# A state-space scan with gated output and attention: y, rows and gate loaded at other places of the loop, mixing split in two

## The reference, cut to what matters

```python
xn = (xc - mu) / jnp.sqrt(var + 1e-05) * ln_g + ln_b        # xc: conv and silu of x @ W_in
Bm, Cm, dt = jnp.split(xn @ W_xproj.T, 3, axis=-1)
def step(h, inputs):
    ad, bd, xt, ct = inputs
    h = jnp.clip(h * ad[:, :, None] + bd[:, :, None] * xt[:, None, :], -10.0, 10.0)
    return h, jnp.einsum('bd,bdh->bh', ct, h)
_, ys = jax.lax.scan(step, h0, (Ad, Bd, xn, Cm))
y = ys + D * xn
x = x + y * jax.nn.silu(gate) @ W_out.T
x = x + attention_layer(x)
```

## Time and profile before

| | us |
|---|---|
| median of 3 runs | 2897.28 |
| lowest, highest | 2895.61, 2928.46 |
| the profiled execution | 2895.71 |
| its span | 2893.9 |
| scan, first to last VectorE step | 466.6 to 1454.99 |

### The profile page before, as it was taken

The page is one execution under the profiler, slowest core; times in us unless marked ns, Lnnn a source line. Parts: engine busy times, 40 slices in busy tenths (PEclk is TensorE's granted clock), DMA queues, the critical chain, the costliest instruction groups (busy, mean ns, idle before and its releaser), DMA issues. The chain is left out here.

```text
span 2893.9 us, 55595 instructions
## 1 busy us (share of the span) xinstructions
PE 2689.5 (93%) x20489; PEld 1466.8 (51%) x20490; DVE 2001.7 (69%) x2112; ACT 1189.3 (41%) x2039; POOL 1281.7 (44%) x583
## 2 busy tenths in 40 slices
PE   7999955999999999999979999969999999999999
PEld 3444333666666665666657777833333333333337
DVE  2788867987888878888853333366777677676726
ACT  2677762221222212122132122126666666666641
POOL 0000002655555555555541222026667777777763
PEclk9999967999999999999989999979999999999999
DMA  3246576878887888888744444372344354354347
GB/s 106 88 154 219 181 257 142 186 164 156 165 162 168 165 155 157 159 162 166 156 141 165 139 143 158 142 200 66 74 110 111 89 128 108 95 126 118 81 173 228
DMA packets 260356, 424.01 MB, mean 147 GB/s; under 512 B 59440, under 2 KB 127664, under 8 KB 253824
## 3 DMA queue, kind: packets, MB, share of 16 engines
q1 hardware_dynamic: 177920, 332.86, 44.5%
q10 hardware_dynamic: 82304, 89.44, 12.7%
HBM read 260.91 MB, written 163.08 MB: 147 GB/s over the span
## 5 line engine op out<-in xcount | busy, mean ns | idle before, releaser
L939 DVE CUSTOM_DVE_ANT_0 b_h<-b_h,b_bx,b_bounds_all 128x512 f32<-128x512 f32 x1024 | 825.7, 806 | 167.1 <-PE b_bx L1087 118.0
L1643 DVE TENSOR_REDUCE e_half_max<-ef_banks 128x4 f32<-128x2048 f32 x256 | 586.3, 2293 | 233.3 <-PE ef_banks L1596 233.3
L1786 POOL TENSOR_TENSOR e_pair_sum<-e_probs 128x2048 f32<-128x2048 f32 x128 | 585.7, 4576 | 264.9 <-PE ef_banks L1635 215.1
L1755 ACT ACTIVATE e_probs<-ef_banks 128x512 f32<-128x512 f32 x1024 | 555.7, 595 | 309.9 <-PE ef_banks L1610 309.9
L1610 PE MATMUL ef_banks<-e_qs,e_ks 97*128 97x512 f32 x1024 | 382.0, 452 | 3.9 <-DVE e_half_max L1643 3.6
L1143 ACT COPY d_v_rows<-b_y_psum 128x128 f32<-128x128 f32 x256 | 67.9, 265 | 690.3 <-PE b_y_psum L1097 690.3
L1087 PE MATMUL b_bx<-b_x_moving,b_b_weights 24*128 24x512 f32 x1024 | 260.4, 504 | 78.1 <-DMA b_x_moving<-xn_parts 46.7
L1610 PEld LDWEIGHTS ef_banks<-e_qs,e_ks 97*128 97x128 f32 x1024 | 154.5, 188 | 330.9 <-ACT e_probs L1755 312.4
L1067 POOL TENSOR_TENSOR b_b_weights<-b_bd,b_mask_b 128x512 fp32r<-128x512 f32 x64 | 82.4, 1287 | 512.9 <-POOLq L861 462.8
L1097 PE MATMUL b_y_psum<-b_h,b_c_weights 128*32 128x128 f32 x8224 | 279.8, 277 | 0.5 <-ACT d_v_rows L1143 0.5
L1620 PE MATMUL ef_banks<-e_probs,e_v 128*32 128x512 f32 x2048 | 273.6, 606 | 0.4 <-ACT e_probs L1755 0.4
(11 more groups left out here) (225 smaller groups left out, 4105.8 us busy)
## 6 DMA issues: line engine op xcount, KB each, us to landing
b_x_moving<-xn_parts SPq DMA_DIRECT2D x252, 128.0 KB
e_ks<-qk_parts ACTq DMA_DIRECT2D x42, 512.0 KB, 4.9
e_qs<-qk_parts ACTq DMA_DIRECT2D x84, 256.0 KB, 3.4
xn_full<-a_xn SPq DMA_DIRECT2D x32, 512.0 KB, 3.3
xn_parts<-a_hi SPq DMA_DIRECT2D x64, 256.0 KB, 2.5
xn_parts<-a_lo SPq DMA_DIRECT2D x64, 256.0 KB, 2.5
silu_gate<-d_v_rows ACTq DMA_DIRECT2D x64, 256.0 KB, 5.6
shared<-xn_full SPq DMA_DIRECT2D x128, 128.0 KB, 5.9
```

The lines of the kernel that those rows point to most:

```text
L939: return nc.vector._custom_dve(bass.dve_ops.TENSOR_ADD_SAT, **operands)
L1643: nc.vector.tensor_reduce(out=half_max[:, u // UNITS % 2, :, r // NH, r % NH], in_=(banks[:, u % 2 * GROUP:(u % 2 + 1) * GROUP] if u < FIR ...
L1755: nc.scalar.activation(probs[:, g % 4, h, :], p_exp[h % 2], ACT.Exp).then_inc(exps, 1)
L1786: nc.gpsimd.tensor_tensor(out=pair_sum[:, t % 2], in0=probs[:, (2 * t) % 4], in1=probs[:, (2 * t + 1) % 4], op=ALU.add).then_inc(paired, 1)
```

## The change

SP: load_y handles tile it-2 and stands behind load_moving half 0 and load_bd; it additionally waits for `gated` of the tile before. load_xn moves from there to a place behind load_sg, after the loads of half 1. GpSimd: mix is cut into scale_rows (xn * D), add_y (plus y) and gate_rows (times the gate). scale_rows of tile it-1 stays at the end of the iteration; add_y and gate_rows of tile it-2 come between split_low and low_turned of the same tile. The ends of the loops follow. In the phase before, spread_early stands at the end of a round and not at the start of the next.

```diff
--- before.py
+++ after.py
@@ -343,8 +343,6 @@
                 for b in range(BATCH):
                     pj.load_style(sp, b)
                 pj.load_others(sp)
-            if p >= 2:
-                spread_early(sp, p - 2)
             if p >= 1:
                 store_b(sp, p - 1, 0, b_hi)
                 store_b(sp, p - 1, 1, b_lo)
@@ -359,6 +357,8 @@
                         for j in "wu":
                             pj.load_mat(sp, mat_of[j], j)
                 store_inverse(sp, p)
+            if 1 <= p <= 2:
+                spread_early(sp, p - 1)
 
         def in_proj(pe, n, m):
             i = n * NM + m
@@ -923,6 +923,7 @@
                 sp.wait_ge(sg_out[half], START + j * 16 + 16)
             sp.dma_start(sg_in, SG[bass.ds(j, 1)].rearrange("o p c -> (o p) c")).then_inc(sg_back, 16)
         def load_y(sp, j):
+            sp.wait_ge(gated, START + j)
             for i in range(2):
                 sp.wait_ge(y_out[i], START + j * 64 + 64)
             for b in range(BATCH):
@@ -938,13 +939,14 @@
         def add_clipped(**operands):
             return nc.vector._custom_dve(bass.dve_ops.TENSOR_ADD_SAT, **operands)
 
-        def mix(e, engine, j):
-
+        def scale_rows(e, engine, j):
             e.wait_ge(xn_in, START + j * 64 + 64)
             engine.tensor_tensor(out=xn, in0=xn, in1=d_row, op=ALU.mult).then_inc(mixed, 1)
+        def add_y(e, engine, j):
+            e.wait_ge(y_in, START + j * 64 + 64)
             e.wait_ge(mixed, START + j * 2 + 1)
-            e.wait_ge(y_in, START + j * 64 + 64)
             engine.tensor_tensor(out=xn, in0=xn, in1=y[:], op=ALU.add).then_inc(mixed, 1)
+        def gate_rows(e, engine, j):
             e.wait_ge(mixed, START + j * 2 + 2)
             e.wait_ge(sg_back, START + j * 16 + 16)
             e.wait_ge(turned, START + j * 2)
@@ -1024,14 +1026,13 @@
 
 
 
-        def sp_loop(sp, it, store=True, x=True, more=True, load_d=False):
-            j = it + (-1)
+        def sp_loop(sp, it, y=True, store=True, more=True, load_d=False):
             sp.wait_ge(read, START + it * PAIRS + 8)
             load_moving(sp, it, 0)
             sp.wait_ge(w_ready[1], START + it * 2 + (-1))
             load_bd(sp, it, 1)
-            if not load_d:
-                load_xn(sp, j)
+            if y:
+                load_y(sp, it + (-2))
             sp.wait_ge(read, START + it * PAIRS + 16)
             load_moving(sp, it, 1)
             if more:
@@ -1041,40 +1042,42 @@
             if load_d:
                 sp.wait_ge(out_split, START + 4)
                 sp.dma_start(d_row, I["D"].rearrange("(o n) -> o n", o=1).to_broadcast([P, INNER])).then_inc(out_in, 16)
-                load_xn(sp, j)
-            load_sg(sp, j)
-            load_y(sp, j)
+            load_sg(sp, it + (-1))
+            load_xn(sp, it + (-1))
             if store:
-                store_x1(sp, j + (-2))
-            if x:
-                load_x(sp, j + (-1))
-
-
-        def pool_loop(pool, it, j, out=False, split=True, low=False, split_out=False):
-            for i in range(2):
-                if i == 1 and split:
-                    split_low(pool, it)
-                if i == 1 and split_out:
-                    for c in range(4):
-                        out_low_part(pool, c)
-                if i == 1 and low:
-                    low_turned(pool, j + (-1), 0)
-                t0 = it * STEPS + i * T
-                pool.wait_ge(read, START + it * PAIRS + (10 + 8 * i))
-                pool.wait_ge(bd_in[i], START + it * 16)
-                bt = bd[:, i, :].rearrange("k (t o d) -> k t o d", o=1, d=STATES).to_broadcast([P, T // PHASES, 8, STATES])
-                mb = mask_b[:].rearrange("k (o r d) -> k o r d", o=1, d=STATES).to_broadcast([P, T // PHASES, 8, STATES])
-                nc.gpsimd.tensor_tensor(out=b_weights[:, i].rearrange("k t (r d) -> k t r d", d=STATES), in0=bt, in1=mb, op=ALU.mult).then_inc(w_ready[i], 1)
-                cc = c_all[:, bass.ds(t0, T)].rearrange("p (t o) -> p t o", o=1).to_broadcast([128, T, 32])
-                nc.gpsimd.tensor_tensor(out=c_weights[:, i], in0=cc, in1=mask_c[:], op=ALU.mult).then_inc(w_ready[i], 1)
+                store_x1(sp, it + (-3))
+            if y:
+                load_x(sp, it + (-2))
+
+
+        def tables(pool, it, i):
+            t0 = it * STEPS + i * T
+            pool.wait_ge(read, START + it * PAIRS + (10 + 8 * i))
+            pool.wait_ge(bd_in[i], START + it * 16)
+            bt = bd[:, i, :].rearrange("k (t o d) -> k t o d", o=1, d=STATES).to_broadcast([P, T // PHASES, 8, STATES])
+            mb = mask_b[:].rearrange("k (o r d) -> k o r d", o=1, d=STATES).to_broadcast([P, T // PHASES, 8, STATES])
+            nc.gpsimd.tensor_tensor(out=b_weights[:, i].rearrange("k t (r d) -> k t r d", d=STATES), in0=bt, in1=mb, op=ALU.mult).then_inc(w_ready[i], 1)
+            cc = c_all[:, bass.ds(t0, T)].rearrange("p (t o) -> p t o", o=1).to_broadcast([128, T, 32])
+            nc.gpsimd.tensor_tensor(out=c_weights[:, i], in0=cc, in1=mask_c[:], op=ALU.mult).then_inc(w_ready[i], 1)
+
+        def pool_loop(pool, it, turn=True, out=True, split_out=False):
+            tables(pool, it, 0)
+            split_low(pool, it)
+            if split_out:
+                for c in range(4):
+                    out_low_part(pool, c)
+            if turn:
+                add_y(pool, nc.gpsimd, it + (-2))
+                gate_rows(pool, nc.gpsimd, it + (-2))
+                low_turned(pool, it + (-2), 0)
+            tables(pool, it, 1)
             if out:
-                add_x(pool, nc.gpsimd, j + (-2))
-            if low:
-                low_turned(pool, j + (-1), 1)
+                add_x(pool, nc.gpsimd, it + (-3))
+            if turn:
+                low_turned(pool, it + (-2), 1)
             if split_out:
                 pool.wait_ge(out_in, START + 32)
-            if j is not None:
-                mix(pool, nc.gpsimd, j)
+            scale_rows(pool, nc.gpsimd, it + (-1))
 
         def products_bx(pe, it, v):
             i, k = v // (PAIRS // 2), v % (PAIRS // 2) // 2
@@ -1166,21 +1169,25 @@
                 sp.wait_ge(w_ready[0], START + 1)
                 load_bd(sp, 1, 0)
                 sp_loop(sp, 1, False, False, load_d=True)
-                sp_loop(sp, 2, False)
+                sp_loop(sp, 2, store=False)
                 with sp.Fori(3, LOOPS - 1) as it:
                     sp_loop(sp, it)
                 sp_loop(sp, LOOPS - 1, more=False)
+                load_y(sp, last - 1)
+                load_sg(sp, last)
                 load_xn(sp, last)
-                load_sg(sp, last)
                 sp.wait_ge(y_free, START + LOOPS * (STEPS // 4) + 1)
                 send_y(sp, LOOPS - 1, 1, range(2, 4))
             @block.gpsimd
             def _(pool):
-                pool_loop(pool, 0, None, split=False)
-                pool_loop(pool, 1, 0, split_out=True)
-                pool_loop(pool, 2, 1, low=True)
-                with pool.Fori(2, TILES - LAG) as j:
-                    pool_loop(pool, j + LAG, j, True, low=True)
+                for i in range(2):
+                    tables(pool, 0, i)
+                pool_loop(pool, 1, False, False, split_out=True)
+                pool_loop(pool, 2, out=False)
+                with pool.Fori(3, LOOPS) as it:
+                    pool_loop(pool, it)
+                add_y(pool, nc.gpsimd, last - 1)
+                gate_rows(pool, nc.gpsimd, last - 1)
             @block.tensor
             def _(pe):
                 with pe.Fori(0, OUT_LAG) as it:
@@ -1265,7 +1272,9 @@
             @block.vector
             def _(dve):
                 add_x(dve, nc.vector, last - 2)
-                mix(dve, nc.vector, last)
+                scale_rows(dve, nc.vector, last)
+                add_y(dve, nc.vector, last)
+                gate_rows(dve, nc.vector, last)
                 pj.split_low(dve, 0)
                 add_x(dve, nc.vector, last - 1)
                 pj.stats_of(dve, 0, early_tiles[:3])
```

## The result

The changed kernel takes 2975.67 us at the median (2966.31 to 2976.2, 4 runs), the kernel before 2899.32 (4 runs). The ratio is 1.0226, with a 95% interval of 1.0171 to 1.0281: slower, by 77 us at the medians. The interval excludes no change; whether the loss is over 2% it leaves open. It is wide because one of the four runs of the kernel before took 2928.46 us, the others 2895.61 to 2901.35. The prediction was 2949, within 2866 to 3000, with 0.43 on slower by over 2% and 0.50 on within 2%. The profiled execution took 2975.86 us (span 2974.1), 80.2 more than before.

What follows compares the result with a forecast made beforehand. Bound: VectorE's chain of scan steps, stalled beyond 28.4 us per undisturbed iteration (the excess). Excess 12.2 - 7.8 = 4.4 us x 30 = 132, less 79 now = +53; 2895.7 + 53 = 2949 us, range 2866 to 3000.

Steps and rivals of the forecast that it cites:

- t0: In each scan iteration, the end of the TensorE readout that permits SP to load x's first half; times count from it.
- part 1: SP's queue: the wait for y's stores disappears, x's first half is issued 4.6 us earlier, TensorE's 2.07 us wait goes.
- part 2: TensorE's turn waits for y's load, add and gate; excess 4.4 us per iteration against 79 us in all now: +53 us.
- y at t0 + 12.2: GpSimd's add_y: tile it-2's y is loaded 12.2 us after t0 in each iteration.
- L: Landing time of the last of y's four loads, from its start at t0 + 6.7: taken as 5.5 us.
- the turn's due time: On TensorE, when the turn would start without a stall: t0 + 14.4.
- 1.5 us for the slow clock: TensorE after its pause before the turn: running at 1.2 GHz instead of 2.4 adds 1.5 us per iteration.
- the gap before a first product: VectorE's idle gap before an iteration's first product, named as a sign of the predicted delay: 0.5 to 1 us.
- the gap before the second pair: VectorE's idle gap before an iteration's second pair of steps, named as a sign of the predicted delay: 3 to 5 us.
- xn and gate later, GpSimd's order, the first phase, the end: 0: Later xn and gate loads, reordered GpSimd work, copies before the scan and the last tiles: each expected to cost 0.
- The faster rival: y lands as in the quiet stretch, t0 + 9.8: -19 us, 2877, or 2832 with the fast clock; chance 0.15.
- Crowding: y's last DMA is as slow as xn's, L = 8.3, y at t0 + 15: +137 us, 3033; chance 0.22.

Runs made afterwards that it cites:

- e10: Kernel before, with only xn's load moved behind the loads of x's second half and of the gate: 2922.78 us, ratio 1.0067.
- e3: Changed kernel, with y's load ahead of SP's wait for x's first half, and add_y and gate_rows ahead of split_low on GpSimd: 2850.12 us, ratio 0.9808.
- e7: Kernel before, with the gate's product on GpSimd done twice per tile, 2.39 us more work: 2877.43 us, ratio 0.9915.
- e2: Changed kernel, with y's load ahead of SP's wait for the permission to load x's first half: 2867.56 us, ratio 0.9882.
- e4: Changed kernel, with the first turn on TensorE at pair 2 instead of pair 0: 2895.12 us, ratio 0.9979.
- e6: Changed kernel, with the gate's product on GpSimd done twice per tile, 2.39 us more work: 3040.01 us.
- e5: Changed kernel, with the two gate pieces of pair 0 ahead of the first turn on TensorE: 2900.15 us, ratio 0.9992.
- e1: Changed kernel, with spread_early put back in its old place before the scan: 2973.31 us.
- e8: e3 with the two gate pieces of pair 0 ahead of the first turn on TensorE, as in e5: 2849.23 us, ratio 0.9798.

## Why the prediction was right, and where it was off

1. *SP's wait goes, x starts at t0* (part 1): 298.5 us became 2.0, and the wait for x_moving is gone. Right. That x was late by SP's late start and not by its neighbour xn was assumed; e10 supports it, and so does e3, where x is late again as soon as SP starts it late. A share of xn of some tenths of a us isn't excluded (e7). That SP's wait could not stay was right for this place by a small margin only: e2 and e3, which ask for y's stores before x is permitted, wait for them again.

2. *y becomes what is late, and the turn pays* (part 2): right. The turn waits 30 times, and e2, e3, e4 and e6 move the time by moving the start, the length and the end of this chain.

3. *y at t0 + 12.2*: add_y starts at t0 + 12.2 in the mean, the turn at t0 + 17.3, both as predicted. L was 5.5; the median landing of y's four loads is now 4.9 us from their issue, where it had been 2.9. That the value came out to the tenth is luck: no row gave it, it was chosen between 3 and 10 us, and e4 shows the same loads arriving some 5 us later. Only the turn's due time was read 0.2 us too late. It was taken from an iteration at the slow clock; at full clock the first product is done, and the turn could start, at t0 + 14.2 (1063.58 + 0.49 - 1049.85) and not 14.4. The wait is thus 3.1 us in the mean instead of 2.9: 6 us in 30 iterations.

4. *1.5 us for the slow clock*: this term was mis-sized. The excess is 5.3 us, the wait 3.1, so the rest is 2.2. It was read from one pause of 2.07 us, after which the clock was up again before pair 1's product (1017.72, 0.50 us long), and 3.84 us passed from the turn's start to VectorE's next pair. After the pause of 3.39 us that product still ran at the slow clock (0.79), and it is 1072.00 - 1067.46 = 4.54. 0.7 us per iteration, 21 us. With point 3: 27 us, which is what lies between +53 and +80. e5 shows the term by itself: with the clock up, 51.4 us of it are gone. The sign that was named for the gap before a first product, 0.5 to 1 us, didn't come (there is none), and the gap before the second pair is larger, 5.4 us in the mean instead of 3 to 5, by this same term.

5. *xn and gate later, GpSimd's order, the first phase, the end: 0*. The first phase is shown by e1. The end too is as long as before: from the scan's last step to the end of the span 1438.9 us (2893.9 - 1454.99) and now 1438.8 (2974.1 - 1535.26). One cost of GpSimd's new order was missed, though it stayed hidden: split_low waits for ScalarE now, 96.1 us in 30 iterations, because it is asked for earlier than x_hi is ready. The prediction had it done at t0 + 7.1; it ends at 1060.26, t0 + 10.4, 2.1 us before y. It came to light in e2, where it set the mixing.

The faster rival needed y by t0 + 10.4 and fell with that, as the earliest is t0 + 11.3. Crowding (third rival) needed y at t0 + 15 and is not what the changed kernel suffers: the latest is t0 + 12.8, and DMA is less loaded in it, at a share of 0.72 over the scan instead of 0.81. Something like it shows in e4, with y at 16.0 us after x's first issue. e3's remainder is not crowding but SP's late start of x.

The best version is e3, or e8, equal to it within their spread: 2850 us, 1.9% faster than the kernel before and 4.2% than the changed one. It keeps the change and adds y's load ahead of x's, and the mixing ahead of split_low, in time in which GpSimd waits. Its price is that x starts at t0 + 5.1 again; no run has the mixing ahead and x first.

## What to carry to other kernels

A wait that is taken from a queue leaves what stood behind it earlier and what it delivered later in the program's order: follow the delivered tile to its reader and count the chain again, from the event that starts it. Here the mixing lost a cover of 7.8 us to save a late start of 4.6. When two loads share a permission, look which has the longer chain behind it, and whether it can go ahead of the permission (e2); then look again at what its own wait does to the load behind it, as here that wait made x late once more. And when an in-order engine must wait, look first for independent work to put ahead of the wait.

## What the runs showed that I had not expected

A pause of TensorE costs more than its length, and how much more doesn't follow from its length. In iterations 3 to 31 of the changed kernel the waits of the turn are 2.2 to 3.7 us long. Beyond its wait an iteration lost 0.1 us once (the wait of 2.87 us at 1269, after which the clock stayed at full speed), 1.4 to 1.6 us eight times, and 2.3 to 2.9 us twenty times. A wait of 3.60 us is among the eight and one of 2.76 among the twenty. What differs is for how long the granted clock stays at 0.50 behind the wait, in the iteration shown until the readout at 1072. A term read from one pause is thus a draw from these values.

y's flight goes with the length of the iteration before: 11.1 to 12.6 us from x's first issue in the changed kernel's iterations of 31 to 34 us, 13.5 to 17.2 after one of 28.4 in e4.

2.39 us of additional work on GpSimd per tile made the kernel before 23 us faster (e7). What it shifted (xn's load 70.4 us later in total, less waiting for x and y's stores, a flight of x of 10.3 us instead of 10.9) is in the trace; what causes what is open.

The early load of y brought the wait for its stores back: 156.1 us in e2, 180.0 in e3, against 2.0 where y's load stands behind x's.
